# Attention's adjacency loads: issued by GpSimd behind its masks instead of by SyncE between its transposes

## The reference, cut to what matters

```python
def _gat_layer(x, W, adj):                    # twice, with W_stack[0] and W_stack[1]
    Wh, Ws = jnp.split(x @ W, 2, axis=-1)     # values and keys, 512 columns each
    a = softmax(Wh @ Ws.T, axis=-1) * adj     # the mask comes after the softmax
    return leaky_relu(a @ Wh + x, 0.01)

x = layernorm(x + gat(gat(x)))
x = layernorm(x + relu(adj @ (max(sign(x), 0) @ sign(weight).T)))
```

## Time and profile before

| | |
|---|---|
| median of 3 runs | 2333.96 us |
| profiled execution: its time, and its span | 2334.25 us, 2332.3 us |
| TensorE matmul busy | 2217.7 us, 95% |
| VectorE busy | 1089.7 us, 47% |
| ScalarE busy | 562.4 us, 24% |
| GpSimd busy | 439.2 us, 19% |
| DMA from SP and ACT, share of the 16 DMA engines | 52.4% (SP), 1.8% (ACT) |
| DMA from POOL, share of the 16 DMA engines | 5.2% |

### The profile page before, as it was taken

How to read it: one execution, slowest core, us unless ns; L and a number is a source line. 1 busy time by engine, 2 the same in 40 slices (tenths; PEclk the granted TensorE clock), 3 DMA queues, 4 the chain that set the end, 5 groups by cost and what they waited for, 6 DMA issues and landing times. The chain is left out here.

```text
span 2332.3 us, 29117 instructions
## 1 busy us (share of the span) xinstructions
PE 2217.7 (95%) x10532; PEld 1037.2 (44%) x10532; DVE 1089.7 (47%) x2243; ACT 562.4 (24%) x881; POOL 439.2 (19%) x241
## 2 busy tenths in 40 slices
PE   3998999999999999997997999999999999998699
PEld 1443444444444444443444444444444444443244
DVE  2434665565556556654433434434444443443254
ACT  5332222122212221222332222222122122121000
POOL 0001222122212212220001331232232232131000
PEclk9999999999999999998998999999999999999799
DMA  7425654564465446534425776766866866874775
GB/s 235 93 62 142 145 120 106 135 144 105 111 144 138 99 122 144 128 94 114 93 61 143 157 157 160 178 148 152 185 143 151 189 147 148 182 158 105 245 248 181
DMA packets 557830, 333.24 MB, mean 143 GB/s; under 512 B 487056, under 2 KB 493840, under 8 KB 556944
## 3 DMA queue, kind: packets, MB, share of 16 engines
q1 hardware_dynamic: 549040, 296.76, 52.4%
q0 software_dynamic: 1248, 22.15, 5.2%
q10 hardware_dynamic: 7488, 13.63, 1.8%
HBM read 211.48 MB, written 46.01 MB: 110 GB/s over the span
## 5 line engine op out<-in xcount | busy, mean ns | idle before, releaser
L599 PE MATMUL p_scores_a<-keys_t,q_t_a 128*128 128x512 f16 (+1 forms) x4368 | 893.4, 366 | 23.0 <-DVE row_a L712 13.2
L614 PE MATMUL p_out_a<-values,probs_t_a 128*128 128x512 f16 x4056 | 883.7, 379 | 0.0
L692 POOL TENSOR_TENSOR kept_probs_a<-row_a,adj_row_a 128x896 f32<-128x896 f32 x208 | 424.6, 2055 | 1615.2 <-ACT row_a L659 1520.7
L599 PEld LDWEIGHTS p_scores_a<-keys_t,q_t_a 128*128 128x128 f16 x4368 | 429.2, 98 | 489.3 <-DVE row_a L712 14.1
L614 PEld LDWEIGHTS p_out_a<-values,probs_t_a 128*128 128x128 f16 x4056 | 396.9, 98 | 467.9
L659 ACT ACTIVATE row_a<-row_a,shift_a,scales 128x896 f32<-128x896 f32 x208 | 222.5, 1071 | 994.7 <-DVE shift_a L722 994.7
L712 DVE TENSOR_SCALAR_CACHE_REDUCE row_a<-p_scores_a 128x512 f32<-128x512 f32 (+1 forms) x364 | 237.1, 653 | 479.3 <-PE p_scores_a L599 472.6
L727 DVE SCALAR_TENSOR_TENSOR row_a<-kept_probs_a,row_a 128x896 f16<-128x896 f32 x208 | 239.6, 1152 | 281.0 <-ACT row_a L674 276.7
L674 ACT ACTIVATE row_a<-kept_probs_a 128x896 f16<-128x896 f32 x208 | 186.1, 895 | 229.4 <-POOL kept_probs_a L692 229.4
L923 PE MATMUL p_out_b<-products_b,adj_b 128*128 128x512 f16 x676 | 149.4, 385 | 24.1 <-issue 24.1
L384 PE MATMUL p_values_p<-w_p,x_t_p 128*128 128x512 f16 x624 | 141.9, 388 | 30.9 <-DMA x_t_p<-x_p 30.9
(11 more groups left out here) (83 smaller groups left out, 599.1 us busy)
## 6 DMA issues: line engine op xcount, KB each, us to landing
adj_row_a<-adj_rows SPq DMA_DIRECT2D x104, 448.0 KB, 4.8
adj_row_a<-adj_rows SPq DMA_DIRECT2D x104, 384.0 KB, 4.3
adj_t<-adj_blocks POOLq DMA_DIRECT2D x26, 832.0 KB, 8.8
adj_b<-adj_t SPq DMA_DIRECT2D x26, 832.0 KB, 4.5
x_rows_a<-x_rows SPq DMA_DIRECT2D x52, 256.0 KB, 3.0
rows_p<-x_rows SPq DMA_DIRECT2D x13, 512.0 KB, 5.2
x_rows_p<-x_rows SPq DMA_DIRECT2D x26, 256.0 KB, 3.2
x_mid<-y_rows_a SPq DMA_DIRECT2D x26, 256.0 KB, 2.4
```

Of the source, the lines that this page charges most:

```text
L599: last = pe.matmul(p_scores[:, bank, 0:widths[k]], q_t[:, b, qh, c, :], keys_t[:, kh, c, k * BANK:k * BANK + widths[k]], start=(n == 0), s ...
L614: last = pe.matmul(p_out[:, b], piece[:, ph * blocks[part] + j, :], values[:, vh, k, :], start=(k == 0 and n == 0), stop=(k == T - 1 and n ...
L692: pool.tensor_tensor(kept_probs[:, part % 2, 0:blocks[part] * P], row[:, b, cols], adj_row[:, cols], ALU.mult).then_inc(masked, 1)
```

## The change

POOL issues the adjacency loads. The four for tile 0 are the first things that it does in the block, and the load of part p for tile t + 1 stands behind the mask of part p of tile t, with the same two waits as on SP. For this POOL's loop is written out over all tiles. SP's queue keeps everything else in its order.

```diff
             @block.sync
-                def load_adj(t, part):
-                    if from_tile(t, 1):
-                        sp.wait_ge(masked, PARTS * (t - 1) + part + 1)
-                        if first_layer:
-                            sp.wait_ge(adj_checked, PARTS * (t - 1) + part + 1)
-                    cols = columns(part, NP)
-                    sp.dma_start(adj_row[:, cols], adj[bass.ds(t * P, P), cols]).then_inc(adj_loaded[part], 16)
...
-                for part in range(PARTS):
-                    load_adj(0, part)
                 load_x(0)
...
                     for part in range(PARTS):
                         turn_probs(t, b, part)
-                        if before_end(t, 1, T):
-                            load_adj(t + 1, part)
             @block.gpsimd
             def _(pool):
-                for t, b in row_tiles(pool, T):
+                def load_adj(t, part):
+                    cols = columns(part, NP)
+                    pool.dma_start(adj_row[:, cols], adj[bass.ds(t * P, P), cols]).then_inc(adj_loaded[part], 16)
+
+                for part in range(PARTS):
+                    load_adj(0, part)
+                for t in range(T):
+                    b = t % 2
                     pool.wait_ge(pad_zeroed, t + 1)
                     for part in range(PARTS):
                         pool.wait_ge(adj_loaded[part], 16 * (t + 1))
...
                         pool.tensor_tensor(kept_probs[:, part % 2, 0:blocks[part] * P], row[:, b, cols],
                                            adj_row[:, cols], ALU.mult).then_inc(masked, 1)
+                        if before_end(t, 1, T):
+                            pool.wait_ge(masked, t * PARTS + part + 1)
+                            if first_layer:
+                                pool.wait_ge(adj_checked, t * PARTS + part + 1)
+                            load_adj(t + 1, part)
```

## The result

The changed kernel takes 2348.97 us in the median of 4 runs (2348.51 to 2350.62), the kernel before 2334.45 beside it: ratio 1.0064, 95% interval 1.0046 to 1.0081. The forecast was 2338.0 with a range of 2334 to 2345. It is slower, as 42 in 100 had it (54 had it the same), and further than the range reaches. The spans of the two profiled executions, 2346.7 and 2332.3, are 14.4 us apart.

A forecast was written before the change was run, and what follows sets the result against it. TensorE, 95% busy with matmuls, was taken as the bound. Tile 0 of both layers (1.4 + 1.6 = 3.0 us) plus the starts (1.0) gave 4.0 us, forecasting 2338.0 us on the median, range 2334 to 2345.

The forecast's parts named there:

- Where the time would go: In `attend`, extra time can show only where TensorE already waits: the start and tile 0 of each layer.
- the steady state: Tiles after tile 0: an added delay of 1 to 5 us fits the room of 7.2 and 8.4, costing nothing.
- The blocks' starts: Query transposes at each layer's start, with POOL's loads possibly beside them: 0.5 us each, 1.0 in all.
- The rival of crowding: Both layers' starts: POOL's loads delay the query transposes, some 3 us per layer, total 2343 us; chance 24%.
- The sign named for it: Both layers' starts: TensorE's wait for `q_t_a` grows beyond about 5.8 us; over 6 us means the starts were misjudged.
- The first layer's tile 0: Waiting for part 1's check, issuing, and mask 3 beside split 2 delay DVE's chain 0.7 to 1.6 us; taken as 1.4.
- The last layer's tile 0: POOL's own chain is delayed by issues between masks and mask 1 beside split 0: 1.15 to 2.0 us, taken as 1.6.
- The sign named for a wrong c: Last layer's tile 0: masks 0 and 1 further apart than a us.
- c: POOL's delay before its next mask, from own-mask wait and load issue: between 0.56 and 1.86 us, taken as 0.75.
- the bound worked out for the largest c: First layer's tile 0, at 1.86 us of delay per load: split 3 comes 2.6 us late.

The follow-up runs named there:

- the run with waits alone: Kernel before, POOL's loop written out with the changed kernel's waits between its masks, but all loads still on SP: 2335.59 us, ratio 1.0006.
- the run with four loads behind the fourth mask: Changed kernel, tile 0's loads back on SP, each later tile's four loads issued by POOL behind the preceding tile's fourth mask: 2367.1 us, ratio 1.0113.
- VectorE's order in that tile: Kernel before, in tile 0 the reads of tile 1's first four score banks put ahead of the four splits, one each: 2316.07 us, ratio 0.9926.

## Why the prediction was wrong

- **Where the time would go was right.** TensorE waits at tile 0 and at the starts alone, and the steady state has room. Both kernels agree to 0.1 us on the long stretches between. The four places cost 14.3 us where the sum had 4.0.
- **The blocks' starts were the failed step**: "I take 0.5 us for each start", 1.0 in all; measured 8.0. The rival of crowding had place and mechanism right, and its bounds (0.9 to 5.0 for each) held the 3.9 and 4.1; its price was 3 us each. The sign named for it came too: the wait is over 6 us. I chose the low end on one row: POOL's first instruction 6.8 us late in the second projection. That row is of another instruction, the reduction over partitions. POOL's DMA came 0.55 us behind SP's first transpose. The rule I set beside it, of code loaded ahead of a first call (the Trainium skill, GPSIMD Engine Reference, Instruction dispatch), did not bear on an issue of DMAs: the measurement decides. The page on DMA (the Trainium skill, DMA: Bandwidth & Descriptors, Issuing engines are not separate DMA queues) says that issuers share the engines and interleave, and the trace agrees: SP's second transpose landed at 188.53, between POOL's second and third load (187.05 and 188.74), and TensorE's wait was 9.1 us beside the loads, 9.7 behind them.
- **The first layer's tile 0** was the second failed step: it was to be 1.4 and was 4.2, 4.0 of them in the wait. That POOL waits for the check of part 1, and that mask 3 gets beside split 2, was right. Three sizes were not. The check itself was taken to end when it always had, though the first issue moves mask 1 beside split 0 as it does in the last layer, where I had counted that: 1.1 us that stood at nothing. Mask 2 starts 1.2 us behind the check's end, where I had 0.75, and that wait cost 1.1 us for 0.7. And for the overlap of mask 3 and split 2, "In the last layer the mask that lies beside a split takes 2.65 us" was read as a rule that the mask pays. Here the split paid, 1.8 us for the 0.7 that I took, and it was on the chain. The Trainium skill says that GpSimd shares a read and a write interface with VectorE and conflicts with instructions that have two inputs in SBUF (Advanced Engine Details and Errata, GPSIMD Details). The rows agree on which ones: the splits, with two such inputs, rose by 0.57 us on average, the checks, with one, stayed (106.6 us busy in both profiles).
- **The last layer's tile 0** was to be 1.6 (1.15 to 2.0) and was 2.1. The sign named for a wrong c came: masks 0 and 1 are 1.07 us apart, and the gap ahead of mask 3 is 0.90, where c was to be 0.75. Of the 0.90, 0.30 are the wait for POOL's own mask and 0.58 the issue; c had 0.19 for the first.
- **The range.** Every place came out above the figure taken for it: the starts at 3.9 and 4.1 for 0.5, tile 0 at 4.2 for 1.4 and at 2.1 for 1.6. The first layer's tile 0 lies above even the bound worked out for the largest c, 2.6 us and 0.85 for the slower mask. I had let the upper ends of the terms stand for single cases, while all come from POOL's loads and what they move. The sum of the upper ends, 8 for tile 0 and 10 for the starts, would have held the time.

What stays open: what it is in an issue that decides the order. In the changed kernel 23 of 25 splits of 768 that started inside an issue, ahead of its mask, paid as if the mask had been first; without an issue, in the run with waits alone, a mask that followed a split by 0.2 us paid itself in all 25 cases. Open too is why the DMA engines moved so little in the run with four loads behind the fourth mask.

## What to carry to other kernels

Moving DMAs to an idle engine's queue gives up an order. Where SP's queue put the transposes that TensorE waits for ahead of loads that have 18 us to come, a second queue ran both at once, and TensorE got its transposes nearly as late as when they stood behind the loads; issue such loads behind the landing of what is needed first. Where an engine is "idle 80%", look at the one tile in which the pipeline fills: there POOL's chain had no cover, and what gained was VectorE's order in that tile, worth 17.6 us.

## What the runs showed of the hardware that I had not expected

- With four loads and a cast together on POOL's queue, SP's transposes took up to 37.5 us to land and the loads up to 31.9, with the DMA engines busy and 99 GB/s moved; at two of 26 tiles TensorE had to wait.
- A mask on GpSimd and a split on VectorE slow whichever starts second: a mask of 768 columns took 2.52 to 2.65 us for 1.8, a split 2.05 for 0.95. A split that started inside a DMA issue on POOL, ahead of the mask, nearly always paid as the second, and took 2.77 to 3.09. A split that paid ended 0.8 us behind the mask's end, while an issue with no mask behind it cost a split nothing (0.96 us).
- ACT's hardware queue crowded the transposes more (10.4 us of wait) than POOL's (9.1). It started 0.4 us earlier; whether that is the whole reason no run shows.
